# The first layer norm's statistics moved into the first eleven steps of a pipelined attention and expert kernel

## The reference, cut to what matters

```python
x = x + tanh(g_xattn[0]) * xattn(layernorm(x), ctx, ctx, mask, Wq, bq, Wk, bk, Wv, bv, Wo, bo)
#   q, k, v = projections to 16 heads of 8; rope on q and k
#   scores = q @ k.T / sqrt(8); masked; softmax over the 64 keys of a sequence; @ v; @ Wo.T + bo
x = x + tanh(g_ffn[0]) * ffn(layernorm(x), W1, b1, W2, b2, Wr, br)
#   logits = x @ Wr + br; idx = argmax(logits); gate = softmax(logits)[idx]
#   out = gelu(x @ W1[idx] + b1[idx]) @ W2[idx] + b2[idx], times gate   (8 experts, hidden size 512)
# layernorm(x) = (x - mean) / sqrt(var + 1e-5), over the 128 values of a row
```

## Time and profile before

| | before |
|---|---|
| median of three runs | 282.6 us (280.78, 282.6, 283.52) |
| the profiled execution | 282.11 us, of it 280.2 us from first to last instruction |
| PE busy | 231.7 us (83%) |
| PEld busy | 201.9 us (72%) |
| DVE busy | 191.5 us (68%), 639 instructions |
| POOL busy | 182.0 us (65%) |
| ACT busy | 166.5 us (59%) |
| mean granted TensorE clock | 0.989 |

### The profile page before, as it was taken

One profiled execution on the slowest core, in us unless ns is written; L12 is line 12 of the kernel. 1 busy time (PEld: TensorE's weight loads), 2 busy tenths in 40 slices (PEclk: granted clock), 3 DMA queues, 4 the chain that ended last, 5 costly groups with the idle time before them and its releaser, 6 DMA issues.

```text
span 280.2 us, 10498 instructions
## 1 busy us (share of the span) xinstructions
PE 231.7 (83%) x3529; PEld 201.9 (72%) x3529; DVE 191.5 (68%) x639; ACT 166.5 (59%) x482; POOL 182.0 (65%) x222
## 2 busy tenths in 40 slices
PE   1357888989799888788988897797869999999992
PEld 1235677878678777567767676676769899999992
DVE  5535867888989889998678977777477434434431
ACT  1235678878778788566877775626464444444440
POOL 7374765757758889548988677740777377555464
PEclk9999999999999999999999999979999999999997
DMA  7811355627464573513425122133123443210010
GB/s 215 245 23 30 94 149 150 170 34 207 107 148 112 118 202 71 145 21 78 117 47 144 43 46 48 34 91 98 56 81 111 116 121 97 69 57 28 28 33 19
DMA packets 58535, 26.63 MB, mean 95 GB/s; under 512 B 38608, under 2 KB 53989, under 8 KB 58484
## 3 DMA queue, kind: packets, MB, share of 16 engines
q1 hardware_dynamic: 55204, 20.15, 29.4%
q0 software_dynamic: 2272, 4.46, 4.7%
q10 hardware_dynamic: 1008, 1.35, 1.7%
HBM read 16.70 MB, written 5.51 MB: 79 GB/s over the span
## 4 chain that ended last, share of the span: by engine, by line
PE 43%; DVE 18%; POOL 12%; issue 11%; DMA 6%; SPq 5%; ACT 4%; POOLq 1%; DVEq 0%
PE ps L751 12%; PE ps L794 5%; DMA kbd<-kT 4%; SPq L407 4%; PE ps L809 3%; DVE mx L1233 3%; PE ps L732 3%; PE ps L734 2%; PE ps L733 2%; PE ps L784 2%; PE ps L770 2%; POOL rows L513 2%; PE ps L836 2%; POOL rot L546 2%; POOL rot L540 2%
## 5 line engine op out<-in xcount | busy, mean ns | idle before, releaser
L563 POOL DMA_INDIRECT out<-fin,got x39 | 37.9, 972 | 28.1 <-DVE fin L1291 14.5
L1233 DVE TENSOR_REDUCE mx<-ps 128x16 f16<-128x1024 f32 x32 | 39.1, 1222 | 15.0 <-PE ps L809 14.8
L751 PE MATMUL ps<-w_f,hT 128*128 x312 | 44.6, 287 | 0.0
L513 POOL DMA_INDIRECT rows<-x_all,dest_i x32 | 33.3, 1040 | 17.2 <-DVE x_all L1068 9.7
L794 PE MATMUL ps<-vx,pr 128*64 128x32 f32 x1024 | 36.2, 224 | 4.4 <-DVE on L1168 2.4
L794 PEld LDWEIGHTS ps<-vx,pr 128*64 128x64 f32 x1024 | 32.7, 138 | 8.1 <-issue 2.9
L751 PEld LDWEIGHTS ps<-w_f,hT 128*128 128x128 f32 x312 | 37.8, 191 | 0.8
L593 ACT ACTIVATE pr<-ps 128x1024 f32<-128x1024 f32 x32 | 32.7, 1023 | 9.0 <-PE ps L836 8.6
L1291 DVE SCALAR_TENSOR_TENSOR fin<-ps,got 128x128 f32<-128x128 f32 x39 | 13.7, 351 | 35.5 <-PE ps L751 33.0
L540 POOL TENSOR_TENSOR rot<-qk,cf 128x256 f32<-128x256 f32 x32 | 23.4, 732 | 22.0 <-ACT qk L615 15.3
L527 POOL TENSOR_TENSOR stk<-rot,stk 128x256 f16<-128x256 f32 x32 | 21.5, 672 | 22.9 <-DVE stk L1245 22.9
(11 more groups left out here) (158 smaller groups left out, 584.7 us busy)
## 6 DMA issues: line engine op xcount, KB each, us to landing
kbd<-kT SPq DMA_DIRECT2D x128, 32.0 KB
got<-rows SPq DMA_DIRECT2D x39, 72.0 KB, 1.9
w_f<-in_W_rows SPq DMA_DIRECT2D x8, 256.0 KB, 2.9
w_r<-in_W_last_row SPq DMA_DIRECT2D x8, 256.0 KB, 3.3
w_f<-in_L_ffn_W SPq DMA_DIRECT2D x8, 256.0 KB, 5.0
x_all<-in_x SPq DMA_DIRECT2D x3, 512.0 KB, 4.5
xt_all<-in_x_t SPq DMA_DIRECT2D x3, 512.0 KB, 4.8
ct_all<-in_ctx SPq DMA_DIRECT2D x3, 512.0 KB, 4.2
```

The source lines that it names most:

```text
L513: pool.indirect_dma_start(out=rows, out_offset=bass.IndirectOffsetOnAxis(ap=dest_i[:, t:t + 1], axis=0), in_=x_all[:, t, :], in_offset=Non ...
L563: pool.indirect_dma_start(out=out_d, out_offset=bass.IndirectOffsetOnAxis(ap=got_i[:, u % GOT, R_ID:R_ID + 1], axis=0), in_=fin[:, u % FRI ...
L751: mm = pe.matmul(o, hT[:, par, c, :], w2_f[:, bass.ds(e, 1), c, :].rearrange("p o n -> p (o n)"), start=False, stop=(c == FC - 1))
L1233: dve.tensor_reduce(mx[:, t % 2, 0:H], ps_s[:, :].rearrange("p (h k) -> p h k", k=S), AX.X, ALU.max).then_inc(mx_done, 1)
```

## The change

Two tables and one condition change. The same 28 tiles get the same statistics in the loop, in other steps: steps 1, 2, 4, 5, 6, 7 and 8 do 1, 1, 2, 2, 1, 1 and 3 tiles more, step 17 one more, steps 11 to 16 and 18 to 23 do none. The last tile but two (29) is done in step 10, tiles 30 and 31 in step 17. The seven `rstd_of` calls in the loop move from steps 1, 3, 7, 11, 15, 19, 23 to steps 1, 3, 5, 6, 8, 9, 18. On SP the row loads of the last two chunks move from steps 6 and 12 to steps 1 and 4; in step 4 the load stands ahead of the three weight loads of the first expert.

```diff
-        STATS_AT = {i: (4 + 2 * i, 5 + 2 * i) if i < 4 else (i + 8,) for i in range(T - 8)}
-        RSTD_AT = {1: 1, 3: 2, 7: 3, 11: 4, 15: 5, 19: 6, 23: 7}
+        STATS_AT = {0: (4, 5), 1: (6, 7, 8), 2: (9, 10, 11), 3: (12, 13), 4: (14, 15, 16), 5: (17, 18, 19), 6: (20, 21), 7: (22, 23),
+                    8: (24, 25, 26, 27), 9: (28,), 10: (29,), 17: (30, 31)}
+        RSTD_AT = {1: 1, 3: 2, 5: 3, 6: 4, 8: 5, 9: 6, 18: 7}
...
-                if i in (6, 12):
-                    rows_of(3 + (i - 6) // 6)
+                if i in (1, 4):
+                    rows_of(3 + (i - 1) // 3)
```

## The result

Twenty runs of each kernel: the median of before is 281.28 us (279.70 to 283.52), that of the changed kernel 283.26 us (281.04 to 286.26). The ratio is 1.0076, with a 95% interval of 1.0049 to 1.0102. The change costs some 2 us where a gain of 0.3 was forecast. The time lies inside the range given (279.2 to 284.7) and within 1% of before, but on the other side of it. The ratios, their intervals and the mean clocks of this text leave out executions more than 1.5% above the fastest of the same kernel (here one of the twenty changed ones); medians are of all runs.

A forecast was written before the change was run, and what follows sets the result against it. No engine is full, so a cycle between engines sets the pace (4.76 us per step for TensorE and ScalarE). Late gains of 2.7 us less early losses of 2.4 gave 0.3 won, 282.11 to 281.8 us; range 279.2 to 284.7.

The forecast's parts named there:

- Steps 12, 13, 20 and 21: Late steps held by VectorE: each 0.42 us shorter with one tile's statistics gone, 0.84 per pair of steps.
- Steps 14 and 15: Late steps, booked as steps 14 to 16: 0.4 us won, bounds 0.2 to 0.51.
- the pair for steps 18 and 19: GpSimd's `rstd` delays step 19's scores by 1.02 us; step 19 still wins 0.4, bounds 0.3 loss to 0.8 gain.
- SP in step 4: Row load of 512 KB ahead of weights and `kbd`: 1.5 us lost, bounds 0.5 to 3.4.
- The slower rival: The row load in step 4 delays `kbd` in full, 3.4 us, giving 283.7 us; chance 0.2.
- the cover: Early statistics of steps 1 to 6 hidden by step 6's wait for `kbd`; about 0.7 us lost without it.
- Steps 7 and 8: Early steps with more tiles and an `rvar`: 0.6 us longer and 0.80 over; step 8 net 0.3 after step 9.
- The strict reading of the lock: VectorE and GpSimd's shared ports block `rvar` behind `rstd` in steps 7 and 8: 1.6 us more lost, 283.4.
- The removed work was no bound: Rival: TensorE or GpSimd holds the late steps, only early losses of 2.4 stay, 284.5 us; chance 0.1.
- The sign of being wrong: Wrong if step 6's scores wait no longer, VectorE idles before steps 12, 20, 21, or `cand` and `logit` change over 0.5.
- the faster rival: SP's load costs only 0.5 and `cand` in step 20 loses 1.3 of 1.69 us, giving 279.5; chance 0.2.
- The exclusion of VectorE waiting for the rows: Rival ruled out: rows for steps 4 and 8 are loaded over 10 us before VectorE wants them.

The follow-up runs named there:

- x3: The changed kernel with the last row load in step 6 instead of 4 (statistics alone); ratio to before 1.0006, median 281.17 us.
- x4: Before without statistics, `rvar` and `rstd` of tiles 20 to 31, a constant 1 for their `rstd`; ratio 0.9906, median 280.23 us.
- x1: The changed kernel run again unaltered, as yardstick of its group; ratio to before 1.0078, median 283.48 us.
- x2: Before with only the row loads moved, to steps 1 and 4; ratio to before 1.0110, median 285.07 us.
- y3: x2 with step 4 loading only tile 24 (64 KB) and tiles 25 to 31 loaded in step 12; ratio to before 1.0013, median 282.85 us.
- z3: Before with eleven extra `bn_stats` and `bn_aggr` pairs in steps 1 to 8, results unused; ratio to before 1.0030, median 282.29 us.
- y1: x3 with the last group's `rstd` in step 20 instead of 18; ratio to before 0.9937, median 280.45 us.
- z1: The changed kernel with the last group's `rstd` in step 20 instead of 18; ratio to before 1.0060, median 283.12 us.
- y2: Before with an extra unused power over four numbers on GpSimd ahead of step 18's `rstd2`; ratio to before 1.0001, median 281.79 us.
- z2: x2 with the row load of step 4 behind the three weight loads, still ahead of `kbd`; ratio to before 1.0145, median 285.11 us.
- y4: Before with its own schedule: statistics moved into VectorE's idle time, row loads in 1 and 6, `rstd` moved; ratio to before 0.9898, median 279.15 us.
- z4: y4 run again in another group; ratio to before 0.9952, median 279.63 us.

## Why the prediction was wrong

**The sum in two parts.** Without the load of step 4 the forecast gives 1.8 us won (the 0.3 and the load's 1.5); x3 measured 0.2 lost (interval -0.8 to 1.2). The load was forecast at 1.5 and cost 2.0. So most of the error is in the first part, and most of that in the late steps. That the time still fell inside the range is the range's width.

**The late gain: one step wrong, others right by luck.** Steps 12, 13, 20 and 21 were forecast 0.42 shorter each and came 0.53, 0.12, 0.35 and 0.81 shorter, 1.81 against 1.68. The sum fits, the reasons only in part: x4 took the statistics out of step 12 and won nothing there, so the 0.53 are GpSimd's moved `rstd`. Steps 14 and 15 gave 0.59, but steps 16 and 17 took 0.53 back (0.1 was forecast for step 17), and step 23 gave 0.09 of 0.35.

**The step that failed is the pair for steps 18 and 19.** The prediction saw that `rstd` now stands ahead of `rstd2` and that the low half, the transposes and the scores of step 19 wait behind it. It then counted 1.02 us of delay, found that the scores come at 110.95 and booked a gain of 0.4, with a bound of 0.3 for a loss; a loss of 0.40 came. Measured from the mark of step 18, the transposes start 4.01 us after it (111.01 less 107.00) where before they start after 2.63 (107.80 less 105.17): 1.38 later, a third more than counted, as GpSimd's operations ran later behind the mark and the low half took 0.94 for 0.66. The scores end 6.94 us after it, before 4.72: 2.22 later. The missing 0.84 is the half clock that followed TensorE's wait of 1.67 us: the values product took 0.42 longer and the scores 0.44. The prediction had no term for that. All three profiles with this arrangement (changed, x1, x3) show the idle time (1.67, 1.72, 1.72) and the fall of the clock at this place, and none of the eleven others does. In the runs the arrangement is worth 0.7% with x3 and 0.2% with the change; the step is shown by the profiles, its price is not settled.

**The gain booked for step 19 was not there.** It was read from the 6.58 us of before, of which `logit` made 1.20. In x2, y3 and z3, with every late statistic in its place, the step takes 5.80 with a `logit` of 0.35, and in y1, with them gone, 5.90. y1 and z1 win 2.49 and 2.68 us between steps 11 and 23 against before's profile, but z3, which moved nothing there, wins 0.71 as well. So about 1.8 to 2.0 us of late gain belong to the schedule with `rstd` in step 20, and 2.7 was too much; x4's 1.4 to 3.9 allows both. The changed kernel won 1.57 and x3 only 0.12.

**SP in step 4: the term mis-sized.** 1.5 us was taken from bounds of 0.5 to 3.4. x1 against x3 gives 2.0 us, x2 against y3 2.7. The issue cost nothing measurable (0.60 in this place, y3), the data nearly all: the 2.0 us that the prediction had worked out for 512 KB came in full, and it had booked only part of them. The prediction took the low end "because the DMA engines have gaps before the weights begin"; they have, but the row load was issued at 35.98, 0.7 us ahead of the first weights, and used little of them: from 36 to 38 us the DMA share was 0.42, before 0.31. The slower rival, full delay of `kbd` at 283.7, is nearest to what came (283.3), but by luck: its load of 3.4 was too dear, and the late gain it kept was too large. The prediction also followed one reader of the delayed loads only. The other is VectorE's weight splitting in step 6. Before, `w_r` was issued at 37.71 and landed 3.1 us later, at 40.8, and the splitting began at 41.82: 1.0 us of slack. In the changed kernel it landed 5.86 us after its issue, and the chain runs through it.

**Early statistics: sizes about right, the cover not.** Steps 7 and 8 were forecast 0.6 and 0.8 longer and came 0.77 each; step 9 gives back 0.24 of the forecast 0.5. Step 10 is 0.26 longer, which was not in the sum: the `rstd` now in step 9 stands ahead of the low half on GpSimd, for which TensorE waits 0.48 us at 64.60. By step 11 x3, without the load, is 1.70 behind; the forecast was 0.9, or 1.6 with the cover gone. But the cover was the new wait of step 6, and in x3 that is not there, while in the changed kernel part of the early work stands behind it. `rvar` took 0.66 and 0.48 in these steps, where 0.37 was the mean. The strict reading of the lock, 1.6 us more, did not come; these two operations lost 0.4 together.

**The other rivals.** "The removed work was no bound" falls by x4. The sign of being wrong that came is the length of the routing operations: `logit` fell from 1.20 to 0.19 and `cand` from 1.69 to 0.73 (118.12), both by more than 0.5, as the faster rival had it. `cand` is short (0.73, 0.74 and 0.74) only in the three profiles with the late TensorE; in the others it takes 1.62 to 1.78. It paid nothing in step 19, since TensorE was late by then, and in step 20 it is in the shorter step above. The exclusion of VectorE waiting for the rows held: no such wait is in the changed kernel's timeline in steps 4 to 10.

**The bounds.** The bounds of the prediction's terms, added as they are listed, run from 278.4 to 287.8 (the latter with the cover of steps 1 to 6 gone), not from 278.2 to 286.4. Nothing hangs on it.

**The sum, once more, with measured terms:** early statistics 0.8 (z3) to 1.7 (x3's profile), row load 2.0, late gain -2.6 (x4's ratio) to -1.4 (its medians), `rstd` in step 18 0.5 to 1.9. That is 0.7 to 4.2, and 2.0 was measured. The terms one by one are too loose to confirm the total; x3's 0.2 and the load's 2.0 add up to 2.2.

## What to carry to other kernels

When work is taken from the engine that ends a step, ask which engine is next, and how long TensorE will then stand idle in one piece: a microsecond on GpSimd cost nothing measurable in before and up to 0.7% where VectorE's work around it was gone. A load put ahead of others on a full queue costs its data to everything behind it, so list each reader of each load behind it and its slack, not only the one on the chain. And check one-execution profiles for stretches of low clock before comparing their totals, and a long operation in one of them against a second execution before booking its time as a gain.

## What the runs showed of the hardware

**The same idle time is not always followed by a lower clock.** Before has an idle time of 1.67 us in step 12 too, and so has x2. Before, timeline of TensorE and window:

```profile
72.86 0.61 PE L784 MATMUL ps<-ch,stk 128*128 128x128 f16 x8 [1.67 <-POOL stk L527]
...
74.35 0.61 PE L809 MATMUL ps<-kbd,qT 128*64 128x256 f16 x8
```

```profile
74.00:76.00 2.00, 2.00 (x52) 1.79 (x49) 1.93 (x4) 1.90 (x8) 0.86 (x2) 1.00 0.32 99
```

And x2:

```profile
73.14 0.61 PE L784 MATMUL ps<-ch,stk 128*128 128x128 f16 x8 [1.67 <-POOL stk L527]
...
74.94 1.05 PE L809 MATMUL ps<-kbd,qT 128*64 128x256 f16 x8
```

```profile
74.00:76.00 2.00, 2.00 (x37) 1.57 (x34) 1.19 (x4) 1.61 (x6) 1.14 (x2) 0.57 0.28 93
```

The instructions of this stretch are the same in both. Step 12 took 6.14 us in the one and 6.90 in the other, and step 13 5.19 and 5.96. Of seven profiles with this 1.67 the clock fell in two (x2, y3) and not in five (before, x4, y2, z2, z3). At step 6, behind a wait of 1.37 to 1.75 us for `kbd`, it fell in x1 and not in the changed kernel, x2, y3 and z1; behind z2's 2.89 us it fell. In before a wait of 1.61 us at 113.02, behind the mark of step 19, was followed by no fall. So the three falls of three in step 19 go with the arrangement, but what decides between a fall and none is open. A fall lasted about 3.5 us as a rule, and about 7 in three places (x3, z1, z2).

**The mean granted clock of the runs.** Over 78 runs of before it is 0.9926, over 31 of the changed kernel 0.9861, x2 0.9818 (12), x3 0.9880 (12), y1 0.9912 (12), x4 0.9967 (7), y4 and z4 0.9932 (22). A fall of 3.5 us to half is 0.0062 of a span of 280 us (1.75 / 280), so by this estimate the changed kernel has about one more of them per run than before. Within the runs of one kernel, 0.01 of clock goes with 0.87 us of time (0.58 to 1.17, 221 runs). By that slope the changed kernel's 0.0065 is about 0.6 of its 2.0 us, and the rest would be the waits themselves. This is a correlation and no experiment, and it leaves most of the spread between runs of one kernel unexplained.

**One operation, the same work, two lengths.** `logit` in step 19 took 1.20 and 1.19 us in before and z2, and 0.35 or 0.36 in the nine other profiles with no `rstd` in step 18. The scatter that GpSimd runs just ahead took 1.06 us in the first two and 1.30 to 1.57 in the nine. What sets the scatter's length is open.
